# Row denominators by scans of the score rows instead of small matmuls, in a fused gated-MLP and masked-pooling kernel

## The reference, cut to what matters

```
x = x + concat(fc2(gelu(fc1(x))), expert[tok](gelu(fc1(x))))
scores = tanh(x @ W1 + b1) @ v                    # (B, 1024)
mask   = l <= j  |  l >= j  |  l != j             # by type of the batch
p      = softmax(where(mask, scores, -1e30), axis=-1)
x = x + einsum('bjl,bld->bjd', p, x) / count(mask)
```

## Time and profile before

| | |
|---|---|
| median of 3 runs | 788.61 us (788.36 to 788.74) |
| the profiled execution | 789.04 us, of which its span (first to last instruction) is 787.3 us |
| busy in the span | PE 775.7 us, DVE 401.0 us, ACT 379.5 us, POOL 109.3 us |
| granted TensorE clock, mean | 0.997 |
| one loop batch, start to start | 191.4 us |

### The profile page before, as it was taken

The page is one execution under the profiler, slowest core; times in us unless marked ns, Lnnn a source line. Parts: engine busy times, 40 slices in busy tenths (PEclk is TensorE's granted clock), DMA queues, the critical chain, the costliest instruction groups (busy, mean ns, idle before and its releaser), DMA issues.

```text
span 787.3 us, 11528 instructions
## 1 busy us (share of the span) xinstructions
PE 775.7 (99%) x3540; PEld 634.2 (81%) x3540; DVE 401.0 (51%) x711; ACT 379.5 (48%) x641; POOL 109.3 (14%) x150
## 2 busy tenths in 40 slices
PE   8999999999999999999999999999999999999987
PEld 6788888888888888888888888888888888888875
DVE  6864667563443433754535333276254433246766
ACT  6856665443545433543445523446354552344542
POOL 3172221400000111310000022040000002204000
PEclk9999999999999999999999999999999999999999
DMA  6899898877864568868776556886787566697732
GB/s 214 283 337 330 307 342 265 262 233 232 236 181 148 174 201 267 260 209 240 218 228 193 152 197 198 272 257 189 226 262 207 158 188 190 212 282 213 219 101 107
DMA packets 130715, 176.93 MB, mean 225 GB/s; under 512 B 10064, under 2 KB 97632, under 8 KB 130656
## 3 DMA queue, kind: packets, MB, share of 16 engines
q1 hardware_dynamic: 130496, 176.20, 71.4%
q0 software_dynamic: 160, 0.01, 0.1%
HBM read 136.33 MB, written 39.85 MB: 224 GB/s over the span
## 4 chain that ended last, share of the span: by engine, by line
PE 96%; DVE 2%; ACT 1%; DMA 1%; issue 0%; SPq 0%; DVEq 0%
PE y L731 15%; PE y L733 15%; PE y L732 15%; PE hA L731 8%; PE hA L733 7%; PE hA L732 7%; PE hF L731 6%; PE hF L732 6%; PE hF L733 6%; PE j L824 2%; PE j L733 1%; PE j L732 1%; PE j L731 1%; PE j L832 1%; PE j L803 1%; PE j L800 1%
## 5 line engine op out<-in xcount | busy, mean ns | idle before, releaser
L731 PE MATMUL y<-hs,w2c 128*128 128x512 f32 x512 | 201.9, 394 | 0.2
L733 PE MATMUL y<-hs,w2c 128*128 128x512 f32 x512 | 199.6, 390 | 0.0
L732 PE MATMUL y<-hs,w2c 128*128 128x512 f32 x512 | 199.3, 389 | 0.0
L731 PEld LDWEIGHTS y<-hs,w2c 128*128 128x128 f32 x512 | 96.1, 188 | 22.1 <-DVE hs L1214 1.9
L733 PEld LDWEIGHTS y<-hs,w2c 128*128 128x128 f32 x512 | 96.1, 188 | 20.5
L732 PEld LDWEIGHTS y<-hs,w2c 128*128 128x128 f32 x512 | 96.2, 188 | 19.3
L731 PE MATMUL hA<-xch,w1c 128*128 128x512 f32 x252 | 99.9, 397 | 2.4 <-DVE xcl L1214 1.9
L733 PE MATMUL hA<-xch,w1c 128*128 128x512 f32 x252 | 98.4, 390 | 0.0
L732 PE MATMUL hA<-xcl,w1c 128*128 128x512 f32 x252 | 98.4, 390 | 0.0
L721 POOL TENSOR_TENSOR x1T<-x1T,xnl 128x512 f32<-128x512 f32 x24 | 30.8, 1288 | 431.6 <-DVE x1T L1340 431.6
L1006 ACT ACTIVATE hst<-hst,bcol 128x512 f32<-128x512 f32 x62 | 43.9, 721 | 88.3 <-DVE hst L1394 88.3
(11 more groups left out here) (274 smaller groups left out, 1094.5 us busy)
## 6 DMA issues: line engine op xcount, KB each, us to landing
w2c<-w2s SPq DMA_DIRECT2D x114, 384.0 KB, 3.6
w1c<-w1s SPq DMA_DIRECT2D x24, 768.0 KB, 4.5
w2c<-exs SPq DMA_DIRECT2D x114, 128.0 KB, 3.9
w1c<-w1s SPq DMA_DIRECT2D x48, 256.0 KB, 3.5
w1c<-w1s SPq DMA_DIRECT2D x24, 512.0 KB, 4.0
x1T<-in_x SPq DMA_DIRECT2D x32, 256.0 KB, 6.0
w1s<-w1c SPq DMA_DIRECT2D x8, 768.0 KB, 4.0
w2s<-w2c SPq DMA_DIRECT2D x16, 384.0 KB, 4.5
```

Source lines behind the costliest of these rows:

```text
L731: nc.tensor.matmul(ps, ah, bh, start=first, stop=False, skip_group_check=onto)
L732: nc.tensor.matmul(ps, ah, bl, start=False, stop=False, skip_group_check=onto)
L733: return nc.tensor.matmul(ps, al, bh, start=False, stop=last, skip_group_check=onto)
```

## The change

The denominators are computed in the 8×128 layout of the score row. With the running maxima F8 and G8, the sum of exp(score − running maximum) obeys a recurrence (each step multiplies the sum by `decay`, the exp of the difference of neighbouring maxima, and adds a term), which one multiply-add scan on DVE computes forwards and another backwards, over all 8 chunks at once. POOL makes the differences and combines the results (`row_sums`), ACT takes seven exps (`exps_B`, `exps_M`), DVE does two scans and a few small operations. PE keeps one 8×8 matmul (`total`, which shares the chunks' sums) and the transposition of the finished row (`rd`, as `mT` does for the maxima: one in the tail, two in a loop batch). Gone are `sums1`, `den`, B1s, E1 and ones2. The other parts of the pooling stay.

```diff
-          (2, 2): [("mT",)], (3, 0): [("bc", 0), ("bc", 1), ("expE",), ("expPW", 0)], (3, 1): [("sums",), ("sums1",)],
-          (4, 0): [("expPW", 1), ("den", 0, 2)], (4, 1): [("pool", 0)], (4, 2): [("pool", 1), ("den", 2, 4)],
-          (5, 0): [("pool", 2)], (5, 1): [("pool", 3), ("den", 4, 6)], (5, 2): [("pool", 4)], (6, 0): [("pool", 5), ("den", 6, CH)],
+          (2, 2): [("mT",)], (3, 0): [("bc", 0), ("bc", 1), ("expE",), ("expB",), ("expM",), ("scan",), ("expPW", 0)],
+          (3, 1): [("sums",), ("total",)], (3, 2): [("den",)],
+          (4, 0): [("rd", 0, BC), ("rd", BC, CH), ("expPW", 1)], (4, 1): [("pool", 0)], (4, 2): [("pool", 1)],
+          (5, 0): [("pool", 2)], (5, 1): [("pool", 3)], (5, 2): [("pool", 4)], (6, 0): [("pool", 5)],
...
-    ("expPW", 0), ("expPW", 1), ("sums",), ("sums1",), ("den", 0, BC)] + [("pool", c) for c in range(BC)] + [
-    ("den", BC, CH)] + [("pool", c) for c in range(BC, CH)]
+    ("scan",), ("total",), ("expPW", 0), ("expPW", 1), ("sums",), ("den",), ("rd", 0, CH)] + [("pool", c) for c in range(CH)]
...
+            def row_sums(b):
+                twice = lambda t: t[:, :].unsqueeze(1).to_broadcast([CH, 2, P])
+                gate(pool, chain, b * NCHAIN + (BOTH - NCHAIN))
+                nc.gpsimd.tensor_tensor(upto(FS), twice(s8), upto(FG), ALU.subtract).then_inc(den_in, 1)
+                nc.gpsimd.tensor_tensor(decay[:, :, :], short_of(FG), upto(FG), ALU.subtract).then_inc(den_in, 1)
+                gate(pool, den_in, b * NIN + (2 - NIN))
+                gate(pool, chain, b * NCHAIN + (MAX - NCHAIN))
+                nc.gpsimd.tensor_tensor(short_of(FG), short_of(FG), twice(m8), ALU.add).then_inc(den_in, 1)
+                nc.gpsimd.tensor_tensor(m0[:, :], s8[:, :], m8[:, :], ALU.add).then_inc(den_in, 1)
+                gate(pool, den_exp, b * NEXP + (6 - NEXP))
+                gate(pool, den_scan, b * NSCAN + (2 - NSCAN))
+                nc.gpsimd.tensor_tensor(short_of(FG), short_of(FG), short_of(FS), ALU.mult).then_inc(den_in, 1)
...
+                nc.gpsimd.tensor_tensor(m0[:, :], m0[:, :], FG[:, 0:P], ALU.add).then_inc(den_in, 1)
...
+                nc.gpsimd.tensor_tensor(m0[:, :], m0[:, :], FG[:, P + 3:2 * P + 3], ALU.add).then_inc(den_in, 1)
...
-                        nc.tensor.matmul(two, Ph[:, c, :], ones2[:, :], start=True, stop=False)
-                        nc.tensor.matmul(two, Pl[:, c, :], ones2[:, :], start=False, stop=False)
-                        last = nc.tensor.matmul(two, Ws[:, c, :], B1s[:, :], start=False, stop=True)
+                elif task[0] == "total":
+                    pe.wait_ge(den_scan, b * NSCAN)
+                    last = nc.tensor.matmul(bank[0:CH, 0:CH], ones8[:, 0:CH], DG[:, :], start=True, stop=True)
+                elif task[0] == "rd":
+                    pe.wait_ge(den_done, b * NDEN)
+                    last = nc.tensor.matmul(bank[:, 0:CH], m0[:, :], ident[0:CH, 0:CH], start=True, stop=True)
...
+            def exps_B(b):
+                act.wait_ge(den_in, b * NIN + (1 - NIN))
+                nc.scalar.activation(upto(FS), upto(FS), ACT.Exp).then_inc(den_exp, 1)
+                act.wait_ge(den_in, b * NIN + (2 - NIN))
+                nc.scalar.activation(decay[:, :, :], decay[:, :, :], ACT.Exp).then_inc(den_exp, 1)
+                act.wait_ge(chain, b * NCHAIN)
+                nc.scalar.activation(t88[:, :], t88[:, :], ACT.Exp).then_inc(den_exp, 1)
...
+                elif task[0] == "scan":
+                    dve.wait_ge(den_exp, b * NEXP + (2 - NEXP))
+                    nc.vector.tensor_tensor_scan(FS[:, 1:P + 1], decay[:, 0, :], FS[:, 1:P + 1], 0.0, ALU.mult, ALU.add
+                                                 ).then_inc(den_scan, 1)
+                    nc.vector.tensor_tensor_scan(FS[:, 2 * P + 1:P + 1:-1], decay[:, 1, ::-1], FS[:, 2 * P + 1:P + 1:-1], 0.0,
+                                                 ALU.mult, ALU.add).then_inc(den_scan, 1)
+                    dve.wait_ge(den_scan, b * NSCAN + (1 - NSCAN))
+                    nc.vector.tensor_scalar(DG[:, :], ident[0:CH, 0:CH], FS[:, P:P + 1], None, ALU.mult).then_inc(den_scan, 1)
```

More of the change, by code:

```diff
@@ L98 @@
     ("xn", 0), ("xn", 1), ("attn",), ("xn", 2), ("xn", 3), ("score",), ("stats",), ("expE",), ("mT",), ("bc", 0), ("bc", 1),
-    ("expPW", 0), ("expPW", 1), ("sums",), ("sums1",), ("den", 0, BC)] + [("pool", c) for c in range(BC)] + [
-    ("den", BC, CH)] + [("pool", c) for c in range(BC, CH)]
+    ("scan",), ("total",), ("expPW", 0), ("expPW", 1), ("sums",), ("den",), ("rd", 0, CH)] + [("pool", c) for c in range(CH)]
 TAIL_ACT = [("x1", oc) for oc in range(OC)] + [
-    ("xn", 0), ("xn", 1), ("attn",), ("xn", 2), ("xn", 3), ("full", 0), ("full", 1), ("expE",), ("full", 2), ("full", 3),
-    ("exp", 0), ("PW", 0), ("exp", 1), ("sums",), ("sums1",), ("PW", 1)]
+    ("xn", 0), ("xn", 1), ("attn",), ("xn", 2), ("xn", 3), ("full", 0), ("full", 1), ("expE",), ("expB",), ("full", 2), ("expM",),
+    ("full", 3), ("exp", 0), ("PW", 0), ("exp", 1), ("sums",), ("PW", 1)]
 TAIL_DVE = [("ysum", 0), ("ysum", 1), ("x1", 0), ("ysum", 2), ("x1", 1), ("ysum", 3), ("x1", 2), ("x1", 3), ("xn", 0),
[L106 to L110, removed]
+            ("xn", 1), ("score",), ("xn", 2), ("stats",), ("mT",), ("expE",), ("xn", 3), ("bc", 0), ("scan",), ("bc", 1),
+            ("expPW", 0), ("total",), ("sums",), ("expPW", 1), ("den",), ("rd", 0, CH)] + [("pool", c) for c in range(CH)]
+FULL_BEFORE = {("bc", 0): 1, ("bc", 1): 2, ("sums",): 3, ("rd", 0, CH): 4}
 def body(kind):
@@ L871, in job @@
                         own_chunk(kind, b, c, pos)
+                    if c % BC == 0:
+                        pe.wait_ge(Wlo, b * 2 + (c // BC - 1))
+                    if c == 0:
+                        wait_used(pe, kind, b, at(kind, place, ("sums",)))
                     last = nc.tensor.matmul(bank[:, :], Ws[:, c, :], Bs[:, :], start=False, stop=True)
@@ L918, in part @@
                             pe.wait_ge(xfull_done, FULL_BEFORE[task])
[L919 to L924, removed]
+                        for c in range(BC) if task[0] == "rd" else [task[1]] if task[0] == "pool" and task[1] >= BC else []:
+                            own_chunk(kind, b, c, at(kind, "p", ("pool", c)))
                         job(kind, b, "p", task, pos)
@@ L1030, in task_part @@
                 bank = jb[bank_of(kind, pos)]
-                if task[0] in ("xn", "attn", "sums", "sums1"):
+                if task[0] in ("xn", "attn", "sums"):
                     act.wait_ge(job_done, job_of(kind, b, pos) + 1)
@@ L1161, in part @@
                     for task in TAIL_ACT:
-                        task_part(kind, b, "p", task, at(kind, "p", task) if task[0] not in ("full", "exp", "PW") else 0)
+                        task_part(kind, b, "p", task, at(kind, "p", task) if task[0] not in ("full", "exp", "PW", "expB", "expM") else 0)
                     return
@@ L1219, in task_part @@
                 bank, used = jb[bk], bank_read[bk]
-                if task[0] in ("score", "stats", "mT", "bc", "den", "pool"):
+                if task[0] in ("score", "stats", "mT", "bc", "total", "rd", "pool"):
                     dve.wait_ge(job_done, job_of(kind, b, pos) + 1)
```

80 lines of the change are left out of this document (48 added, 32 removed).

## The result

The changed kernel takes **785.19 us** (median of 6 runs, 784.33 to 785.97) where the kernel before takes 788.49 (6 runs beside it): ratio 0.9962, 95% interval 0.9952 to 0.9971. That is 3.3 us or 0.4% faster. A later series gave 785.56 us and 0.9964 (0.9951 to 0.9977). The forecast was 785.0 us. The profiled execution took 784.57 us, with a granted clock of 0.995 (0.997 before).

The account below looks back on a forecast made before the run. PE, working 775.7 of 787.3 us, was taken as the bound. Loop −4.9, tail −0.2 and clock +1.5 gave −3.6 us, from the 788.6 median to 785.0 us; range 782.6 to 786.8.

Parts of the forecast that it names:

- What PE loses and gets in the loop: Loop, PE: 2.90 us a batch removed, 1.28 added by `total` and two `rd`; net gain 1.62 a batch.
- the low bound of 0.3: Loop, PE: lower price in us for `total`, whose weights have 8 columns where `mT` loads 128; 0.52 was taken.
- other small edits: Loop: E1 and B1s gone, two reciprocals for four, pool banks alternating without `den` between; claimed to gain nothing.
- −4.9: Loop: time change in us over three batches from PE's net gain of 1.62 each; gain bounded 4.0 to 5.5.
- 91 instruction rows fewer: PE's program: a sign that would show the prediction, 91 fewer instruction rows on PE.
- Added work hides in the loop: Loop, ACT, DVE and POOL: added work costs nothing; DVE's addition comes 0.9 us later, 1.0 of 1.9 cover stays.
- `total` ahead of the sums: Tail, PE: waits 2.5 to 3 us for DG before `total`, so the chunk sums start 3.2 us later.
- Contention: Tail, DVE: two-input operations slow beside POOL's work ahead of DG; 0.6 us taken, 0 to 1.2.
- The clock: Tail, PE: clock falls to its lower level after PE's gap, adding 1.5 us on the sums; chance 0.50.
- the clock does not fall: Rival, tail: the clock stays full because the early fall need not recur; −5.1, 783.5 us; chance 0.27.
- The chain behind the sums: Tail: sums start at 771.2, first scaling at 779.1, eight scalings take 5.4 us, ending 784.4 against 784.63.
- +1.3: Tail in total, in us: −0.2 from late sums against removed dens, and +1.5 from the clock.

Follow-up runs that it names:

- Experiment 5: Changed kernel with seven more 8×128 exps on ACT in each loop batch, results unused: 787.77 us, ratio 0.9997.
- Experiment 1: Changed kernel with `total` moved behind the 16 matmuls of the chunk sums on PE in the tail: 781.09 us, ratio 0.9904.
- Experiment 6: Changed kernel with four more 8x128 subtractions on POOL in the tail, ahead of its first difference, results unused: 785.14 us, ratio 0.9962.
- experiment 3: Changed kernel with ten filling matmuls of 512 columns on PE ahead of `total` in the tail: 782.36 us, ratio 0.992.
- experiment 4: Kernel before the change, with one matmul a chunk instead of three in the loop's `den`: 784.07 us, ratio 0.9946.
- its repetition: Changed kernel with `total` behind the chunk sums in the tail, run once more beside two variants with an earlier `den`: 781.26 us, ratio 0.9917.

## Why the prediction was right

The mechanism, the sign and the time held (785.0 forecast, 785.19 measured); two sizes were off, in opposite directions.

- **What PE loses and gets in the loop.** Forecast −1.62 a batch, measured −1.95 to −2.04. The two `rd` cost 0.74 (forecast 0.76). `total` cost 0.34, not 0.52: it was taken from `mT`, whose weights have 128 columns, and the low bound of 0.3, named for that reason, was nearer. With these two the sum is −1.82. The rest is a term that the prediction put at nothing, under "other small edits": with product and reciprocal out of the way, DVE's addition behind `pool` 0 no longer holds PE, 0.18 a batch. That gives −2.00 with the rounding of the rows. The term that was mis-sized is "−4.9": it is −5.9. The "91 instruction rows fewer" should be 89 (100 gone, 11 new).
- **Added work hides in the loop.** Right, with its numbers: the exps came to 1.9 us where about 1.7 were taken, the addition kept 1.05 us of its cover (forecast 1.0), no wait of PE appeared. Experiment 5 shows that the cover is real and how it ends.
- **`total` ahead of the sums.** Sums 3.22 us later (forecast 3.2), PE's wait 2.85 (2.5 to 3). Scans at 0.40 and 0.39 (0.41). Experiment 1 shows that the order does it.
- **Contention.** Forecast 0.6, measured 0.7. Behind the marker, mT is copied 0.26 later than before and the first half of `bc` ends 0.54 later (11.45 against 10.91), although DVE has 0.16 less to do for E. The largest piece is the three casts of E, 0.74 where they took 0.30. Experiment 6 shows the mechanism on other operations. The Trainium skill (GPSIMD Engine Reference, Key points) names instructions in a two-port mode beside those with two SBUF inputs; the casts have one input, so only the first half of that rule can cover them, and no run here shows in which mode they ran.
- **The clock.** Forecast +1.5 with 0.50 of the chance, measured +1.80 in the profiled run; experiment 3 takes it away and gets 1.8 back. The rival "the clock does not fall" (783.5 us) was wrong. Its ground was that the fall near the start need not recur; it recurred in both profiles of the changed kernel.
- **The chain behind the sums.** Forecast 7.9 us from the sums' start to the first scaling; measured 9.90, of which 1.80 is the clock: 0.2 too little. The eight scalings took 5.37 (5.4). With the 0.3 on the clock and 0.2 behind the last scaling, whose duration varies, the tail is +2.0 instead of +1.3.

So where did the expected gain go? 5.9 us were won and a third of it, 2.0 us, was given back by one place in a hand-written order: PE was made to wait for DG with 16 ready matmuls behind it, and the wait cost twice, by its length and by the clock. Moving `total` behind `sums` gives the version to keep: **781.1 to 781.3 us**, 0.9904 and 0.9917, about 7 us faster than before and 4 faster than the change.

## What to carry to other kernels

Where one engine is busy throughout, small operations on it are paid in full, each at the distance to the next start; a longer way round over engines with idle time is free up to the cover of the next hand-over, which can be read off the timeline, and is paid one for one beyond it. A hand-over whose cover is used up need not show as idle time: here two starts that took 0.64 us instead of 0.46 were its only sign, and it took a quarter of what experiment 4 should have saved. In a tail the same move needs another order: let the bound engine do what is ready first, and ask for the new result last. A wait in front of dense work can cost a second time, through the clock, and an added load on an idle engine can slow its neighbour.

## What was not expected of the hardware

- The exps of 8×128 with a tile as bias take 0.39 us on ACT, as long as one of 8×256 without (0.40); those of 8×128 without one, in experiment 5, take 0.29 to 0.31, and one of 128×8 takes 0.21.
- DVE operations on only 8 partitions, or of 8 columns, can slow beside POOL as much as large ones: 0.34 us became 0.58 and 0.73 (experiment 6), and three casts of 128×8 took 0.74 instead of 0.30, where a 128×512 went from 0.69 to 1.22.
- The clock fell in one profile of the kernel of experiment 1 (its repetition) at waits of 0.98, 0.35 and 0.41 us with short work between them, and in the other, with the same waits (0.99, 0.35, 0.41), it did not. What decides it stays open.
- PE's matmuls of 2 columns in a stream of full ones cost 0.11 us each, be they two or six in a place (experiment 4 and the earlier trace rows), which is half of a full one's 0.227.
- The granted clock of a window can say 1.00 while the matmuls tell another thing. Near the start of the changed kernel (timeline of PE, then the window):

```profile
8.29 0.63 PE L767 MATMUL hA<-xch,w1c 128*128 128x512 f32 x1
8.72 0.63 PE L765 MATMUL hF<-xch,w1c 128*128 128x512 f32 x1
```

```profile
8.00:9.00 1.00, 1.00 (x4) 1.00 0.88 270
```

Starts 0.43 apart are what the rows of before show at a granted clock of 0.50. Before the first recorded change of the clock, the distance of the starts is the better witness.
